# Expert outputs of a mixture-of-experts stage signalled, weighed and scattered by halves

## The reference

```python
B, S, _ = x.shape
residual = x
h = _rmsnorm(x, norm_w)
flat = h.reshape(-1, H)                      # 1600 tokens x 512
logits = flat.astype(jnp.float32) @ router_w.T
scores = jax.nn.softmax(logits, axis=-1)
topk_w, topk_ids = lax.top_k(scores, K)      # K = 4 of E = 32
topk_w = topk_w / jnp.sum(topk_w, axis=-1, keepdims=True)
...
xs = jnp.take(flat, tok_idx, axis=0)
gu = lax.ragged_dot(xs, w1, group_sizes)     # w1: 32 x 512 x 512
g, u = jnp.split(gu, 2, axis=-1)
act = jax.nn.silu(g) * u
ys = lax.ragged_dot(act, w2, group_sizes)    # w2: 32 x 256 x 512
...
routed = jnp.sum(y.reshape(T, K, H) * topk_w[..., None].astype(ys.dtype), axis=1)
shared = jax.nn.silu(flat @ sg) * (flat @ su) @ sd
out = residual + (routed + shared).reshape(B, S, H)
```

## Time and profile before

| | us |
|---|---|
| median of 3 executions | 1215.94 |
| lowest and highest | 1205.55, 1221.78 |
| profiled execution | 1210.05 |
| its span, first to last instruction | 1208.3 |
| mean granted TensorE clock | 0.983 of full speed |

### The profile page before, as it was taken

One profiled execution on the slowest core, in us unless ns is written; L12 is line 12 of the kernel. 1 busy time (PEld: TensorE's weight loads), 2 busy tenths in 40 slices (PEclk: granted clock), 3 DMA queues, 4 the chain that ended last, 5 costly groups with the idle time before them and its releaser, 6 DMA issues. The chain is left out here.

```text
span 1208.3 us, 21017 instructions
## 1 busy us (share of the span) xinstructions
PE 1146.3 (95%) x7761; PEld 905.7 (75%) x7762; DVE 811.5 (67%) x1392; ACT 595.0 (49%) x1404; POOL 359.2 (30%) x279
## 2 busy tenths in 40 slices
PE   6989999999999999999999989899799999999993
PEld 3457677767776777777677758788699999898992
DVE  1355798789778978887898868532356666666660
ACT  1334564456446544654554435311156666666661
POOL 0011112211221122112122202222226676667653
PEclk9999999999999999999999988999989999999997
DMA  8450000000000000000000005122669999999964
GB/s 276 141 178 11 1 10 9 16 14 9 9 16 14 9 9 14 9 9 16 14 9 9 17 24 191 44 88 67 229 195 266 261 263 265 263 257 240 268 103 53
DMA packets 62598, 117.59 MB, mean 97 GB/s; under 512 B 10932, under 2 KB 14564, under 8 KB 62388
## 3 DMA queue, kind: packets, MB, share of 16 engines
q1 hardware_dynamic: 44820, 82.46, 20.2%
q0 software_dynamic: 17728, 34.44, 14.5%
HBM read 93.55 MB, written 28.13 MB: 101 GB/s over the span
## 5 line engine op out<-in xcount | busy, mean ns | idle before, releaser
L1483 POOL TENSOR_TENSOR rall<-qkv_var,phalf 100x17 f32<-100x17 f32 x16 | 49.1, 3071 | 404.1 <-DVE qkv_var L1163 404.1
L1561 POOL DMA_INDIRECT out_rows<-work,idx x64 | 119.6, 1868 | 110.0 <-issue 55.0
L382 PE MATMUL QS<-xh,wh 128*128 128x256 f32 x512 | 148.6, 290 | 0.0
L383 PE MATMUL QS<-xl,wh 128*128 128x256 f32 x512 | 146.0, 285 | 0.0
L384 PE MATMUL QS<-xh,wl 128*128 128x256 f32 x512 | 145.8, 285 | 0.0
L382 PE MATMUL W<-wch,oth 128*100 128x512 f32 x256 | 105.1, 410 | 0.0
L383 PE MATMUL W<-wcl,oth 128*100 128x512 f32 x256 | 100.6, 393 | 0.0
L384 PE MATMUL W<-wch,otl 128*100 128x512 f32 x256 | 100.4, 392 | 0.0
L382 PEld LDWEIGHTS QS<-xh,wh 128*128 128x128 f32 x512 | 99.4, 194 | 1.2
L383 PEld LDWEIGHTS QS<-xl,wh 128*128 128x128 f32 x512 | 99.4, 194 | 1.2
L384 PEld LDWEIGHTS QS<-xh,wl 128*128 128x128 f32 x512 | 99.2, 194 | 0.0
(11 more groups left out here) (223 smaller groups left out, 2880.9 us busy)
## 6 DMA issues: line engine op xcount, KB each, us to landing
raw<-in_w SPq DMA_DIRECT2D x24, 1024.0 KB
raw<-in_w SPq DMA_DIRECT2D x24, 512.0 KB
work<-in_w SPq DMA_DIRECT2D x8, 1024.0 KB
work<-in_w SPq DMA_DIRECT2D x8, 512.0 KB
hx_rows<-h3x SPq DMA_DIRECT2D x16, 212.5 KB
h_columns<-h3s SPq DMA_DIRECT2D x16, 200.0 KB, 1.9
h3T<-h_columns SPq DMA_DIRECT2D x4, 800.0 KB, 15.5
out_rows<-ytiles POOLq DMA_DIRECT2D x16, 200.0 KB, 2.5
```

The source lines that it names most:

```text
L382: mm(dst, ah, bh, start=start, stop=False)
L383: mm(dst, ah, bl, start=False, stop=False)
L1483: return nc.gpsimd.tensor_tensor(out=dst, in0=src, in1=phalf[:, 0:src.shape[1]], op=ALU.pow)
L1561: nc.gpsimd.indirect_dma_start(out, on_rows(idx[:, NE * j + e:NE * j + e + 1]), Y[e % 2][:, 512 * j:512 * (j + 1)], None, compute_op=ALU.a ...
```

## The change

Instead of once for each expert, the two semaphores between TensorE, ScalarE and GpSimd are raised once for each half. `outer` raises `m.y_ps` after the 6 matmuls of each bank and waits for `m.y_w` separately ahead of each bank. `weigh` waits for each bank's matmuls separately and raises `m.y_w` after each ACTIVATE. `scatter` waits first for the landing of the scatters of the expert before, then ahead of each of its two DMAs for that half of `Y`. All other uses of the two semaphores are counted in halves (`FAST` times as many).

```diff
@@ sync, experts with more than 256 tokens
-                                sp.wait_ge(m.y_ps, NE)
+                                sp.wait_ge(m.y_ps, FAST * NE)
@@ tensor, outer(e)
-                if e > 0:
-                    pe.wait_ge(m.y_w, e)
                 for j in range(FAST):
+                    if e > 0:
+                        pe.wait_ge(m.y_w, FAST * (e - 1) + j + 1)
                     for f in range(FE // P):
                         c, w = slice(256 * f + P * j, 256 * f + P * (j + 1)), slice(2048 + 512 * f, 2560 + 512 * f)
                         last = split_product(wb[j][:, :], eh[:, c], el[:, c], wh[u][:, w], wl[u][:, w],
                                              f == 0, f == FE // P - 1)
-                last.then_inc(m.y_ps, 1)
+                    last.then_inc(m.y_ps, 1)
@@ scalar, weigh(e)
-                act.wait_ge(m.y_ps, e + 1)
                 act.wait_ge(m.wcol, FAST * (e + 1))
                 if e >= 2:
                     act.wait_ge(m.scat_add, 32 * (e - 1))
                 for j in range(FAST):
-                    last = fn(Y[e % 2][:, 512 * j:512 * (j + 1)], wb[j][:, :], ACT.Copy, scale=wcol[e % RING][:, j:j + 1])
-                last.then_inc(m.y_w, 1)
+                    act.wait_ge(m.y_ps, FAST * e + j + 1)
+                    fn(Y[e % 2][:, 512 * j:512 * (j + 1)], wb[j][:, :], ACT.Copy, scale=wcol[e % RING][:, j:j + 1])\
+                        .then_inc(m.y_w, 1)
@@ scalar, ahead of eh
-                    act.wait_ge(m.y_ps, e)
+                    act.wait_ge(m.y_ps, FAST * e)
@@ gpsimd, scatter(e)
-                pool.wait_ge(m.y_w, e + 1)
                 if e > 0:
-                    wait_alone(pool, m.scat_add, 32 * e)
+                    pool.wait_ge(m.scat_add, 32 * e)
                 for j in range(FAST):
+                    wait_alone(pool, m.y_w, FAST * e + j + 1)
                     nc.gpsimd.indirect_dma_start(out, on_rows(idx[:, NE * j + e:NE * j + e + 1]), Y[e % 2][:, 512 * j:512 * (j + 1)],
                                                  None, compute_op=ALU.add).then_inc(m.scat_add, 16)
```

More of the change, by code:

```diff
@@ L769, in _ @@
                                 n = pe.snap(done)
-                                pe.wait_ge(m.y_w, NE)
+                                pe.wait_ge(m.y_w, FAST * NE)
                                 pe.wait_ge(o.y_w, n)
```

## The result

The changed kernel takes 1203.57 us (median of 18 executions, 1197.95 to 1220.56), the kernel before 1209.30 us in the 18 executions beside them (1201.40 to 1222.23). The ratio is 0.9943, with a 95% interval of 0.9915 to 0.9971: faster, clear of noise, and by less than 2%. Of the 11.3 us between my 1214.9 and 1203.57, 6.6 are my starting point, the median of three executions; the change itself was forecast at 1.0 us and brought 5.7. (The means of the two sets, 1211.3 and 1204.3, are 7.0 apart.)

A forecast was written before the change was run, and what follows sets the result against it. TensorE, busy 95%, bounds the kernel, with 7.9 us of stalls, mostly at gathers behind scatters. Earlier scatters give 1.0 us, added waits nothing: 1215.94 - 1.0 = 1214.9 us, range 1203 to 1224.

The forecast's parts named there:

- The added waits: Extra waits on PE, ScalarE and POOL: counted as nothing; upper ends 3.7 us on PE, 0.56 us on POOL.
- the bound of 11.1 us: Most the profile offers: 7.9 us of PE stalls in the expert loop plus 3.2 us in the tail.
- the first rival: The rival "The jump is avoided": 1204.8 us, chance 0.17.
- an advance is carried along: Scatter chain from expert 8 on: an earlier scatter start stays as it is to the end, taken as 1.0 us.
- the 1.0 us: Forecast gain from earlier scatters, gathers and last scatter, chosen between a lower bound of 0 and an upper of 1.64.
- its jump at expert 12: Lag from weighing start to first scatter jumps to 8.6 us there; all PE stalls come after it.
- the 9.34 of my sum: Scatter chain's own step per expert, in us: 1.93 between scatters, 6.55 landing, 0.86 restart.
- The jump is avoided: Rival: the lag never grows past 4 us, so stalls and tail delay go, 11.1 us less, 1204.8; chance 0.17.
- The lag comes early: Rival: first scatters locked in the large split bring the jump at expert 1, + 5.1 us, 1221.0; chance 0.15.
- Given back at once: Rival: full DMA engines land scatters no earlier however early the issue, nothing changes, 1215.9; chance 0.15.
- a satisfied wait costs a restart: Rival: POOL's added wait costs 0.56 us in 25 experts, 14 us, 1229.9; chance 0.05, shared with PE's waits.
- released by the DMA: Expert 5's scatter before the change: the landing taken as its releaser, about as late as the weighing.

The follow-up runs named there:

- z1: The changed kernel with the scatter of expert 12 forced to wait for the second Silu of expert 13 (lag 4.1 us once): median 1218.38 us, ratio 1.0065.
- e2: The changed kernel, weighed by halves, but both scatters wait for the second half: median 1210.13 us, ratio 0.998 to the kernel before.
- e3: The changed kernel with the scatter of expert 12 also forced to wait for Silu of expert 14: median 1218.96 us, ratio 1.0077 to the kernel before.
- e1: The kernel before with only the scatter's two waits reordered, landing first and y_w last: median 1216.59 us, ratio 1.0047.
- x7: The changed kernel with VectorE's splits in pieces of 128x512 and scatters skipping unused places, no forced delay: median 1205.01 us, ratio 0.9940 to before.
- x3: The changed kernel with e3's forced delay and only a quarter of each w2 row loaded from expert 4 on: median 1212.69 us, ratio 1.0032 to before.
- x6: The changed kernel with e3's forced delay, splits in pieces of 128x512 and x3's fewer weights: median 1208.87 us, ratio 0.9979 to the kernel before.

## Why the prediction was wrong

**Right.** The first ACTIVATE runs before TensorE has finished the second half, and the first scatter starts that much earlier (forecast 1.64 us, measured 1.77). Its issue is locked under the large split (2.01 forecast, 2.14 measured), which leaves 1.27 us for the second scatter (1.26). The added waits cost nothing that shows: 0.30 us between issues, PE without a gap ahead of `outer` other than the last, weigh steps of 9.36. The place where the gain would arise, PE's stalls at the gathers and the tail, was the right one, and so was the bound of 11.1 us above it. That 1203.57 lies inside my range, and near the 1204.8 of the first rival, is luck in part, since both stood on a median that was 6.6 us too high.

**The step that failed** is that "an advance is carried along, and neither grows nor shrinks by the halves themselves", and with it the 1.0 us. I took one profiled execution for the kernel, and its jump at expert 12 for something that comes in any case. It comes in some executions and not in others: it begins with a landing that takes 2 to 3 us longer. What comes then depends on the lag that is reached. From the 9.51 us of experts 8 to 11 and the 9.34 of my sum I had concluded that the chain keeps an advance or loses a little of it. The steps of the 17 traces show three regimes instead: under a lag of 3.4 us the mean step is 9.4 us against PE's 9.36, with steps down to 8.0, so a small excursion can come back; from 3.6 to 7 us every step is longer than 10.4, which no excursion survives; and from 8 us on it is 9.7, so that the chain stays there and PE stalls. The room ahead of the point of no return is 3.6 or so less the lag: some 1.5 us before, and with the halves 3.2 at the least lag and 2.7 at the median one. An advance of 1.8 us is worth little as time and much as room. By the counts the share of late executions falls from 0.54 to 0.05 (101 of 186, 2 of 42); at some 10 us each (1217.5 against 1207.3) that is 5 us on the mean. To this come 2.4 us in the tail of the executions that aren't late. The sum, about 6 to 7, is near the 5.7 of the medians and the 7.0 of the means. It is an estimate from counts and not a measurement of its parts.

**The rivals.** "The jump is avoided" was what happened, with a chance of 0.17 from me; its price of 11.1 us was right for a single execution (10.2 by the two medians of before), and it applies to about half of them. My reason against it, that full DMA engines would make the jump anyway, held only for its cause, not for what the chain does with it. "The lag comes early" showed in no profile as early as I had it (expert 1), though the first issue is locked in many early steps as I had feared; the changed kernel's two late executions (1217.74 and 1220.56 us) were not profiled, and z1, the same kernel up to expert 12, had its late chain from expert 9. "Given back at once" and "a satisfied wait costs a restart" are excluded by the rows above. That expert 5 was "released by the DMA" in the kernel before was a misreading: experts 1 to 6 all have the lag of 2.13 or 2.14 us that is weighing and restart alone, so the weighing set it.

**The base.** The spread of the three executions shown (1205.55 to 1221.78) was itself the sign of two kinds of execution: about half of the kernel's own executions lie over 1210 us. I noted the spread and used it only to widen the range.

What stays open: why some landings take longer. The first excursion is not at a different expert each time: in before, after, e2, e3 and z1 it is the landing of expert 6 that is long (7.0 to 7.8 us from the end of the second issue to the next first one, where 5.4 to 5.9 is usual at rest), and no view shows its cause. Also open is why the landing takes over 7 us in all six steps that start at a lag near 4 us. That e1 was slower than before (1.0047) has no explanation here.

## What to carry to other kernels

Where a chain with chance delays runs beside a bottleneck at almost the same step (here 9.4 to 9.7 us on average beside 9.36), ask how late it may be and still come back, and count an earlier start as room for that, not as time. Sorting the chain's steps of several executions by the lag at which they start shows where that point lies. A spread of the executions that is larger than any stall you can name points to such a case: force the delay once, at one place, and see whether the end moves by as much, by nothing, or by more. And if an advance is small, look at the last pass of the loop, where nothing hides it.

## What was not expected of the hardware

A scatter's issue that starts inside VectorE's 128x2048 subtraction ends 1.43 to 1.62 us after the subtraction does, in 36 of 37 cases of the traces of before and of the changed kernel (912.40 + 2.14 is 1.49 after 910.76 + 2.29); the one exception starts 0.01 us into it. One that starts ahead of the subtraction takes its usual time. From the kernel before, DVE and POOL:

```profile
1123.63 2.29 DVE L1431 TENSOR_TENSOR wl<-raw,wh 128x2048 fp32r<-128x2048 f32 x1 [0.23 <-ACT wh L799]
```
```profile
1123.58 1.63 POOL L1561 DMA_INDIRECT out_rows<-work,idx  x1 [2.84 <-issue]
```

The Trainium skill (SBUF — State Buffer, SBUF: two separate sides) says that whichever of the two instructions starts first gets the shared pair of ports for its whole length and the other fully blocks; for a VectorE instruction with two SBUF inputs, as this one has, it says so only against a GpSimd instruction that reads SBUF. The trace agrees for the issue that comes second. It doesn't show the reverse: the subtraction at 1123.63 starts 0.05 us into an issue and neither waits nor takes longer than its 2.29 us. Cutting the subtraction into pieces of 512 columns brought the mean issue of a late chain from 2.12 to 1.70 us, and cost nothing that the ratio of x7 shows. And a quarter less of each expert's weights (221 GB/s in x3 and 234 in x6 from 1060 to 1120 us, against 250 in e3) left the landing of a late chain, on average over experts 13 to 25, at 4.4 us (x3) and 4.7 us (x6) after the second issue's end, against 4.75 in e3: it is not simply the load on the DMA engines that sets it. For experts 26 to 31 of e3, after the last weight loads, it is 3.5 to 3.8 us.
